# Attention kernel: the output product taken for two units at once, written-out orders of TensorE and VectorE, and an fp32 latent stage

## The reference

```python
x = x + 0.5 * ffn(layernorm(x), Wg, Wu, Wd, Wr, temperature)
x = x + attn(layernorm(x), w_down_q, w_down_kv, w_up_q, w_up_k, w_up_v, w_out, ln_scale, ln_bias)
x = x + 0.5 * ffn(layernorm(x), Wg, Wu, Wd, Wr, temperature)

# attn: h is the normed input; 16 heads of 64
c_q = h @ w_down_q.T; c_kv = h @ w_down_kv.T          # latents, 64 wide
q = rope(c_q @ w_up_q.T); k = rope(c_kv @ w_up_k.T); v = c_kv @ w_up_v.T
attn = softmax(q @ k.T / 8)
out = (attn @ v) @ w_out.T + residual
```

## Time and profile before

| | us |
|---|---|
| median of 3 runs | 1767.47 |
| lowest and highest | 1766.25, 1869.04 |
| profiled execution | 1765.87 |
| its span, first to last instruction | 1764.1 |

### The profile page before, as it was taken

How to read it: one execution, slowest core, us unless ns; L and a number is a source line. 1 busy time by engine, 2 the same in 40 slices (tenths; PEclk the granted TensorE clock), 3 DMA queues, 4 the chain that set the end, 5 groups by cost and what they waited for, 6 DMA issues and landing times. The chain is left out here.

```text
span 1764.1 us, 48101 instructions
## 1 busy us (share of the span) xinstructions
PE 1607.9 (91%) x19056; PEld 1014.7 (58%) x19056; DVE 1484.2 (84%) x3091; ACT 1226.4 (70%) x1683; POOL 1307.3 (74%) x912
## 2 busy tenths in 40 slices
PE   3999765999999999999999999999999999967999
PEld 2666531565666665666666665666666666644666
DVE  4888897999999999899999999989999998846763
ACT  3333251888888888888888888888888888863332
POOL 1445424888888888888888888888888887743545
PEclk9999985999999999999999999999999999988999
DMA  5333202111121112111121111111111112002334
GB/s 175 100 100 104 60 1 72 38 37 38 39 52 32 46 29 52 50 38 38 38 52 33 47 29 47 50 43 38 38 46 39 47 29 58 9 2 85 115 109 126
DMA packets 65341, 96.10 MB, mean 54 GB/s; under 512 B 11488, under 2 KB 23776, under 8 KB 64864
## 3 DMA queue, kind: packets, MB, share of 16 engines
q1 hardware_dynamic: 62320, 92.18, 19.1%
q10 hardware_dynamic: 2800, 0.85, 0.2%
HBM read 40.18 MB, written 2.36 MB: 24 GB/s over the span
## 5 line engine op out<-in xcount | busy, mean ns | idle before, releaser
L1233 POOL TENSOR_TENSOR area<-area 128x1024 f16<-128x1024 f32 (+1 forms) x512 | 831.2, 1645 | 168.1 <-ACT area L1196 168.0
L1121 DVE TENSOR_REDUCE area<-ps 128x1 f32<-128x512 f32 x1024 | 654.6, 685 | 66.6 <-PE ps L999 58.9
L1194 ACT ACTIVATE area<-ps 128x1024 f16<-128x1024 f32 x512 | 525.6, 1027 | 217.2 <-PE ps L1026 217.2
L1045 PE MATMUL ps<-cv_all,area 128*128 128x64 f16 x4096 | 458.2, 195 | 0.0
L1043 PE MATMUL ps<-cv_all,area 128*128 128x65 f16 x4096 | 456.5, 193 | 1.5 <-POOL area L1233 1.5
L1047 PE MATMUL ps<-cv_all,area 128*128 128x65 f16 x4096 | 454.9, 192 | 0.0
L999 PE MATMUL ps<-area 128*128 128x512 f16 x1024 | 395.9, 387 | 38.6 <-DVE area L1118 18.1
L1045 PEld LDWEIGHTS ps<-cv_all,area 128*128 128x128 f16 x4096 | 381.3, 97 | 82.2
L1043 PEld LDWEIGHTS ps<-cv_all,area 128*128 128x128 f16 x4096 | 384.8, 97 | 45.0 <-POOL area L1233 1.4
L1025 PE MATMUL ps<-area 128*128 128x512 f16 x1024 | 390.7, 382 | 5.9 <-DVE area L1145 1.7
L1026 PE MATMUL ps<-area 128*128 128x512 f16 x1024 | 389.0, 380 | 0.0
(11 more groups left out here) (160 smaller groups left out, 2277.0 us busy)
## 6 DMA issues: line engine op xcount, KB each, us to landing
area<-area SPq DMA_DIRECT2D x384, 128.0 KB, 2.7
area<-f_w_rows_in_dram SPq DMA_DIRECT2D x128, 256.0 KB, 3.3
xg<-in_x SPq DMA_DIRECT2D x4, 512.0 KB, 7.4
out_x<-xg SPq DMA_DIRECT2D x3, 512.0 KB, 4.5
area<-in_wup SPq DMA_DIRECT2D x1, 1024.0 KB, 8.0
cs<-in_rope SPq DMA_DIRECT2D x1, 1024.0 KB, 8.7
area<-area SPq DMA_DIRECT2D x64, 2.0 KB
area<-in_wo ACTq DMA_DIRECT2D x1, 512.0 KB, 6.7
```

Of the source, the lines that this page charges most:

```text
L1045: nc.tensor.matmul(o[:, 0:DH], p_hi[:, s % 4, c:c + P], latents[:, DH + 1:CV], start=False, stop=False, skip_group_check=True)
L1121: nc.vector.tensor_reduce(mx[:, hd, kh, qt:qt + 1], bank, AX.X, ALU.max).then_inc(s_mr, 1)
L1194: nc.scalar.activation(p_hi[:, s % 4, :], sc, ACT.Exp, scale=0.125).then_inc(s_e16, 1)
L1233: nc.gpsimd.tensor_tensor(p_lo[:, s % 4, c0:], src[:, (s // 2) % 2, :], p_hi[:, s % 4, c0:], ALU.subtract).then_inc(s_pp, 1)
```

## The change

Output product: an OP item is now worked in even units only (from unit 2), and its tile sums the products of two units, 24 instead of 12. The transposed context is kept for two units (`a` in the tiles below). VectorE's add to the residual comes once for two units.

Orders: two tables of 16 words, one per step, write out TensorE's queue (x and y are the two halves of the scores, p and q those of pv, the rest are items) and VectorE's (L is `low`, S the reciprocal of the row sums, C the product with it, t the subtraction after the cast of T). Items move between steps, pv may stand ahead of the scores, and S and C are apart, with items between them.

Latent stage: the latents are fp32 products of `h32` with fp32 weights, 2 of 512 columns and 4 of 64 per quarter, with no fp16 pairs; ScalarE writes `h32` from PSUM with scale and bias, so that VectorE's L820 and GpSimd's L848 are gone. The down-projection weights are loaded twice, by four DMAs for two, and no longer split (`down_high`, `down_low`).

```diff
@@ load, first feed-forward stage
-            act.dma_start(st_dn[:, 0:64], wdq).then_inc(s_small, 16)
-            act.dma_start(st_dn[:, 64:128], wdkv).then_inc(s_small, 16)
+            for r in range(2):
+                act.dma_start(wdn[:, 0, r, :], wdq).then_inc(s_small, 16)
+                act.dma_start(wdn[:, 1, r, :], wdkv).then_inc(s_small, 16)
...
-                        v.wait_ge(s_small, 112)
+                        v.wait_ge(s_small, 144)
@@ latent stage, VectorE
                 for q in range(NQ + 1):
-                    some_norm(3)
+                    some_norm(6)
                     if q < NQ:
-                        v.wait_ge(s_yT, q + 1)
-                        if q >= 2:
-                            v.wait_ge(s_hlo, q - 1)
-                        nc.vector.tensor_scalar(h32[:, q % 2, :], ps[:, q % 2, :], lnsb[:, 0:1], lnsb[:, 1:2],
-                                                ALU.mult, ALU.add).then_inc(s_h32, 1)
-                        some_norm(3)
@@ latent stage, ScalarE
-                    act.wait_ge(s_h32, q + 1)
+                    act.wait_ge(s_yT, q + 1)
...
-                    nc.scalar.copy(hh_hi[:, q % 2, :], h32[:, q % 2, :]).then_inc(s_hhi, 1)
+                    nc.scalar.activation(h32[:, q % 2, :], ps[:, q % 2, :], ACT.Identity, scale=lnsb[:, 0:1],
+                                         bias=lnsb[:, 1:2]).then_inc(s_h32, 1)
@@ latent stage, TensorE
                     for k in range(2):
-                        for m, (w_, a_) in enumerate(((0, a_hi), (0, a_lo), (1, a_hi))):
-                            last = nc.tensor.matmul(ps[:, bank + k, :], wd2[:, k, w_, :], a_, start=(m == 0), stop=(m == 2))
-                        last.then_inc(s_lat, 1)
+                        nc.tensor.matmul(ps[:, bank + k, :], wdn[:, k].rearrange("p r n -> p (r n)"), h32[:, q % 2, :],
+                                         start=True, stop=True).then_inc(s_lat, 1)
                     for j in range(4):
...
+                        last = nc.tensor.matmul(ps[:, bank + 2, DH * j:DH * j + DH], h32[:, q % 2, P * j:P * j + P], wdn[:, 1, 0, :],
+                                                start=(j == 0), stop=True, skip_group_check=True)
@@ attention, the tables
-        plan = {s: [letters[c].pop(0) for c in step] for s, step in enumerate(
-            "aa aaaa Tm Tbb r rPb Pbb bbbb bb bbbb bcn cccc r rcc cc c".split())}
+        of_letter = {c: list(tiles_) for c, tiles_ in letters.items()}
+        pe_order = ("apxaayq axpayaq xTpymq xTpqby xbpryPrq pxyqb xbypq bPpbxbybqb xbybpqb xpbyq bcxbpbyq pncxcyrqc xypq ccxpqcry pxcyqc cxpyq").split()
+        dve_order = ("aaa LaSaCa TtLm Ttb brPLrS b Cb LbPbbbb bLSbb Cb bcbbL nccrc L cccrS cLc cC").split()
+        plan = {s: [letters[c].pop(0) for c in step if c not in "xypq"] for s, step in enumerate(pe_order)}
...
-            return [i for i in plan[s] if (2 * u + i[1] < CHUNKS if i[0] == "R" else i[1] <= left)]
+            return [i for i in plan[s] if (2 * u + i[1] < CHUNKS if i[0] == "R" else u > 0 and u % 2 == 0 if i[0] == "OP" else i[1] <= left)]
@@ attention, TensorE
-                            a = [c_[:, 4 * i + t, :] for c_ in (cxt_hi, cxt_lo)]
-                            for m, (x_, y_) in enumerate(((0, 0), (0, 1), (1, 0))):
-                                last = nc.tensor.matmul(bank[:, P * t:P * t + P], a[x_], (wc_hi, wc_lo)[y_][:, w % PAIRS, :],
-                                                        start=(t == 0 and m == 0), stop=(m == 2), skip_group_check=True)
+                            for a in range(2):
+                                pair = (w - 1 + a) % PAIRS
+                                c_ = [x_[:, a, 4 * i + t, :] for x_ in (cxt_hi, cxt_lo)]
+                                for m, (x_, y_) in enumerate(((0, 0), (0, 1), (1, 0))):
+                                    last = nc.tensor.matmul(bank[:, P * t:P * t + P], c_[x_], (wc_hi, wc_lo)[y_][:, pair, :],
+                                                            start=(t == 0 and a == 0 and m == 0), stop=(a == 1 and m == 2),
+                                                            skip_group_check=True)
...
-                        for c in "wiwiwiwiii":
+                        for c in pe_order[s]:
+                            if c in work:
+                                work[c]()
+                            elif todo and todo[0] in of_letter.get(c, ()):
...
@@ attention, VectorE
                     elif kind == "OT":
...
-                        nc.vector.tensor_copy(cxt_hi[:, c_, :], both).then_inc(s_oh, 1)
-                        v.wait_ge(s_oh, u * 2 + (i + 1))
-                        nc.vector.tensor_tensor(cxt_lo[:, c_, :], both, cxt_hi[:, c_, :], ALU.subtract).then_inc(s_mr, 1)
+                        nc.vector.tensor_copy(cxt_hi[:, w % 2, c_, :], bank.rearrange("p (t n) -> p t n", t=4)).then_inc(s_oh, 1)
...
+                        grp = (u, s // 4 - 1) if s > 3 else (u - 1, 3)
+                        for c in dve_order[s]:
+                            if c == "L":
+                                low(u * STEPS + (s + 1 - s % 2), s + 1 - s % 2)
+                            elif c == "S":
+                                if u > 0 or s > 3:
+                                    row_sums(*grp)
+                            elif c == "C":
+                                if u > 0 or s > 3:
+                                    context(*grp)
+                            elif c == "t":
+                                context_low(converted, u, 1 - par)
```

More of the change, by code:

```diff
@@ L737, in turn @@
                         if first and last:
-                            for k in range(4):
-                                after_[9 + k].append(lambda k=k: down_low(v, k))
                             for k in range(13):
@@ L897, in _ @@
                     bank = 2 + 3 * (q % 2)
-                    pe.wait_ge(s_hlo, q + 1)
+                    pe.wait_ge(s_h32, q + 1)
                     if q >= 2:
                         pe.wait_ge(s_llo, 3 * (q - 1))
-                    a_hi, a_lo = hh_hi[:, q % 2, :], hh_lo[:, q % 2, :]
                     for k in range(2):
-                        for m, (w_, a_) in enumerate(((0, a_hi), (0, a_lo), (1, a_hi))):
-                            last = nc.tensor.matmul(ps[:, bank + k, :], wd2[:, k, w_, :], a_, start=(m == 0), stop=(m == 2))
-                        last.then_inc(s_lat, 1)
+                        nc.tensor.matmul(ps[:, bank + k, :], wdn[:, k].rearrange("p r n -> p (r n)"), h32[:, q % 2, :],
+                                         start=True, stop=True).then_inc(s_lat, 1)
                     for j in range(4):
-                        cols = slice(P * j, P * j + P)
-                        for m, (a_, w_) in enumerate(((a_hi, 0), (a_hi, 1), (a_lo, 0))):
-                            last = nc.tensor.matmul(ps[:, bank + 2, DH * j:DH * j + DH], a_[:, cols], wd2[:, 1, w_, 0:DH],
-                                                    start=(j == 0 and m == 0), stop=(m == 2), skip_group_check=True)
+                        last = nc.tensor.matmul(ps[:, bank + 2, DH * j:DH * j + DH], h32[:, q % 2, P * j:P * j + P], wdn[:, 1, 0, :],
+                                                start=(j == 0), stop=True, skip_group_check=True)
                     last.then_inc(s_lat, 1)
@@ L1086, in unit, with second_half @@
+                                scores(v_, k_, t, t % 2)
+                            def second_half(t=t, v_=v_, k_=k_, g=g):
+                                if t % 2:
+                                    pe.wait_ge(s_pd, (g + 1) // 2)
+                                scores(v_, k_, t, 1 - t % 2).then_inc(s_s, 1)
+                            work["x"], work["y"] = first_half, second_half
                         if g > 0:
                             u_, k_, s_ = (u, k, s - 1) if s > 0 else (u - 1, 1 - k, STEPS - 1)
-                            work += [lambda u_=u_, k_=k_, s_=s_: pv(u_, k_, s_, 0),
-                                     lambda u_=u_, k_=k_, s_=s_: pv(u_, k_, s_, 1).then_inc(s_pv, 1)]
+                            work["p"] = lambda u_=u_, k_=k_, s_=s_: pv(u_, k_, s_, 0)
@@ L1090, in unit @@
+                            work["q"] = lambda u_=u_, k_=k_, s_=s_: pv(u_, k_, s_, 1).then_inc(s_pv, 1)
                         todo = items(s, left)
[L1091 to L1093 removed]
+                        for c in pe_order[s]:
+                            if c in work:
+                                work[c]()
+                            elif todo and todo[0] in of_letter.get(c, ()):
@@ L1094, in unit @@
                                 misc(todo.pop(0), u, k, n, par, ot_read)
                                 n, par = n + 1, 1 - par
-                            if c == "w" and work:
-                                work.pop(0)()
+                        assert not todo
                 n = run_units(prologue, unit)
@@ L1165, in context @@
```

(22 more changed lines are left out.)

65 lines of the change are left out of this document (16 added, 49 removed).

## The result

| | us |
|---|---|
| before, beside it on the same chip | 1767.34 |
| after, median of 4 runs | 1681.64 (1681.26 to 1684.64) |
| ratio, with its 95% interval | 0.9521 (0.9502 to 0.9539) |
| span of the profiled execution | 1679.5 (before 1764.1) |

One execution of the kernel before took 1869.04 us, far from all its others, and is not in the ratio. Faster by 4.8%, against 1709 forecast, in the range of 1680 to 1742 but close to its lower end: the time of rival B, 1682. In the latent stage ScalarE's `h32` is L844, the fp32 products are L868 and L871.

The account below looks back on a forecast made before the run. No engine was taken as full: TensorE and VectorE, both near it, stop each other through two shared banks. From 1765.9 us, attention's 51 and the latent stage's 6.5 come off and the tail adds 1: 1709, range 1680 to 1742.

Parts of the forecast that it names:

- rival B: Attention: nearly all TensorE stalls go, 78 us, and 7 in the latent stage: 1682 us; chance 0.17.
- What bounds the kernel: Attention: TensorE works 36.9 of 39.8 us a unit, idle 2.9; VectorE 35.5; no engine full, each stops the other.
- The walk: Attention: new orders followed with trace pitches, leaving TensorE stalls of 0.9 us in an even unit, 1.0 in an odd one.
- It knows no jitter, so I add 0.4: Attention: 0.4 us a unit added to the walked stalls, so idle falls from 2.9 to 1.3.
- the three of 0.1 in steps 7 to 10: Attention, 12 b tiles in steps 7 to 10: remaining TensorE stalls of 0.1, 0.1 and 0.1 us.
- The merge: Attention, output product every second unit: VectorE loses one add, 0.6 us a unit; worth between 0 and 0.6.
- S and C: Attention: splitting them hides the product's wait for the reciprocal behind a reduction, 4 times under 0.2 us.
- Rival C: Attention: pv ahead of the scores waits for GpSimd's low part, making it slower: 1819 us; chance 0.08.
- Rival A: Attention: stalls only move and only the adds go, 19 us, with 6 from the latent stage: 1741; chance 0.22.
- The latent stage: Latent stage: L820 leaves VectorE, 0.75 us a quarter; gains 3.8, 0.8 and 2, together 6.5 us; range 0 to 10.
- The fp32 products: Latent stage, TensorE: an fp32 product of 512 columns taken as 0.5 us, against 0.645 for the three fp16 replaced.
- Rival D: Latent stage: fp32 products are dear, so it gives nothing or loses 3 us: 1717; shares the forecast's 0.53.

Follow-up runs that it names:

- e2: Kernel before with only the output product for two units every second unit, old orders and old latent stage: 1761.54 us, ratio 0.9968.
- e3: Changed kernel with the output product back in every unit, 12 products a tile: 1698.22 us, ratio 0.9612.
- e6: Changed kernel with VectorE's reciprocal moved down right ahead of its product, no item between them: 1695.31 us, ratio 0.9594.
- e10: Kernel before with pv ahead of the second half of the scores in odd steps: 1783.79 us, ratio 1.0094.
- e7: Changed kernel with a piece of TensorE's work moved between two A tiles in each of steps 0, 10 and 15: 1689.82 us, ratio 0.9559.
- e9: Changed kernel with e7's three moves and the transpose n behind the first c tile in step 11 on both engines: 1697.47 us, ratio 0.9602.
- e1: Kernel before with the fp32 latent stage alone, attention untouched: 1756.69 us, ratio 0.9946.

## Why the prediction was right or wrong

*What bounds the kernel.* Right in kind: TensorE's own work and what remains of its idle. The work was put somewhat too high. The transposes of OT follow each other by 0.109 us, 0.9 a unit for 8 and not 1.1; with that and 0.0307 for a pv product it is about 36.6, so that the idle of a unit before was 39.8 - 36.6 = 3.2 us and not 2.9.

*The orders.* The walk gave 0.9 us of stalls in an even unit and 1.0 in an odd one. Measured by the distances of M: even 38.65 - 36.6 - 1.3 = 0.7, odd 36.13 - 36.6 + 1.3 = 0.8. So the walk's sums were right within 0.2. The step that failed is "It knows no jitter, so I add 0.4": from unit to unit of one kind the distance of the M tiles varies by 0.03 us (one unit was 0.3 longer, and the first and the last two have fewer items), and there is no jitter to add. With the 2.9 for 3.2 that makes 1.65 forecast and 2.4 measured (39.82 - 37.39) a unit, or 51 us against 72.1 in all. The saving of the stalls was named right at the places: no wait of over 0.3 us of VectorE for an A tile, 8.7 for 74.1 of the scores for the low part, a remaining stall of 0.3 in step 10. The small terms are another matter: the three of 0.1 in steps 7 to 10 are not in the trace, 0.1 ahead of n and, in odd units, 0.1 between two halves of the scores were not in the walk, and some 0.2 is spread in pieces too small to place. That the sums agree so closely is in part luck. The forecast's own sign for B (a pitch under 37.5) came, and so did its sign of being wrong, an even and an odd unit together under 75 us: 74.8. B's sum met the time with one term too large and one too small: it has 78 and 7 us for attention and the latent stage, where 72.1 and 11.5 were measured.

*The merge.* Between 0 and 0.6 a unit, said the text: measured 0.30 (e2) and 0.41 (e3).

*S and C.* I put them at "4 times under 0.2, already in the walk". e6: 0.39 a unit.

*Rival C*, pv ahead waiting for GpSimd, did not come. L1211 waited 49.6 us for ScalarE (35.9 and 13.7), 102.2 before, and GpSimd is busy 94% of attention without being late. It is near: the odd units of 36.13 us leave 0.9 over its 35.2.

*Rival A*, stalls that only move, is false of the change as a whole and true of pieces tried by themselves: e10 in the kernel before, e7 and e9 in the changed one. Its sign did come, A tiles' waits for reductions that grow as others shrink (32.5 to 56.8 us), and so was no sign of A: those are waits of weight loads, which cost TensorE hardly anything.

*The latent stage.* 6.5 us forecast, 10.2 to 11.5 measured. I counted L820's time alone. The step that failed is "L820 leaves VectorE, 0.75 a quarter. In five quarters that is the pitch": it left out that L848, which goes too, held VectorE up for about a microsecond in each of the first five quarters. The rows stood in the trace of before, and I had not compared two durations of one line. ScalarE's `h32` starts at 219.75, 223.75, 227.17, 230.59 us: 4.0 and then 3.4, where 5.0 and 3.4 were forecast. In e1 the 4.0 is 5.3.

*The fp32 products* were mispriced, and the Trainium skill's rule, which I had set aside with the earlier trace rows, was right. Groups of TensorE in the changed latent stage, and its timeline:

```profile
L868 PE MATMUL ps<-area,w_down_twice 128*128 128x512 f32 x32 | 16.0, 624 | 0.0
```

```profile
225.18 1.88 PE L868 MATMUL ps<-area,w_down_twice 128*128 128x512 f32 x4
226.90 1.00 PE L871 MATMUL ps<-w_down_twice,area 128*128 128x64 f32 x8
```

The code has 16 such products and the trace 32 records: one fp32 product shows as two. So 225.18 to 226.90 are two products, 0.86 us each, four times the 0.215 of one fp16 product. My 0.5 came from "eight fp32 products took 1.14 us" in the earlier trace rows, which were four. The rule (the Trainium skill, FP8 and Floating Point Precision, TensorE Precision Notes) says four passes, and 0.86 is what I had worked out from it. At full clock it cost next to nothing: a quarter's fp32 work on TensorE, with 0.84 for the four narrow ones and 0.44 for the transposes, is 3.0 us, and the quarter takes 3.4. At the low clock it did cost. In e1 the first such products fell into it (0.5 granted), two in 3.42 us, and ScalarE stood for them:

```profile
218.96 3.62 PE L868 MATMUL ps<-area,w_down_twice 128*128 128x512 f32 x4
...
222.62 0.58 ACT L833 CAST xt_lo<-ps 128x512 f16<-128x512 f32 x1 [1.12 <-PE ps L868]
```

In the changed kernel the same four records took 2.45 us. The granted clock of the latent stage was 0.94 there and 0.88 in e1, and its length 31.0 and 32.3 us; the other kernels with this stage, at 0.87 to 0.90, took 31.9 to 32.8. Rival D's mechanism was true, and its price, as far as these runs show it, was 1 to 2 us.

*The loads* and the tail: the first feed-forward stage took 0.9 us less (the latent stage starts at 214.5 us, 215.4 before), less than it varies by between kernels, and from the last M to the last add it is 32.0 us against 31.6, where 1 was allowed.

## What to carry to other kernels

When two engines trade tiles through a few buffers, walk both queues with pitches from the trace, and believe the walk more than a margin added on top: its sum was right within 0.2 us in 37, where a list of waits gave the wrong sign for the piece with TensorE's largest wait. Change both queues together, since half of a good pair of orders can be slower than none. Before a gap counts as a stall, count the instructions around it against the program's, and do the same for the number of records that one product leaves.

## What the runs showed of the hardware that I had not expected

VectorE's small instructions of the norm, from SBUF to SBUF and 0.16 or 0.34 us long, took 0.96 to 1.34 us where GpSimd's of 1.15 to 1.3 us ran beside them; a reduction of one SBUF tile did not (0.17). An fp32 product of 512 columns costs 0.86 us at full clock and 1.71 at the low one and leaves two records; an fp32 transpose of 128 columns costs 0.109 and leaves one. And the granted clock of the first stage differs between profiled executions of code that is the same up to there (0.91 or 0.96 from 20 to 100 us), which moves the total by up to 4 us with no change in the stage that was changed.
